# A decoder layer on one core: the order of work in 39 expert tiles, weights split one unit ahead, gate and up signalled apart

## What is computed

```
x = layernorm(x + self_attention(x))                  # 16 heads
x = layernorm(x + cross_attention(ctx, x))
X = x + attention(rmsnorm(x))
h2 = rmsnorm(X)                                       # 4096 tokens x 256
topw, topi = top_k(softmax(h2 @ router_w), 2)         # 2 of 8 experts for each token
shared = swiglu(h2, sh_gate, sh_up, sh_down)
spec   = sum over e of combine[:, e] * swiglu(h2, e_gate[e], e_up[e], e_down[e])
out = layernorm(x + X + shared + spec)
# swiglu(x, g, u, d) = (silu(x @ g) * (x @ u)) @ d ; g, u: 256 x 512, d: 512 x 256
```

## Time and profile before

| | |
|---|---|
| runs | 1156.73 us median of 3 (1155.41 to 1157.38) |
| profiled execution | 1154.84 us, span 1153.0 us |
| TensorE busy | 1076.8 us, 93% of the span |
| VectorE, ScalarE, GpSimd busy | 805.8, 620.1, 551.0 us |
| units 0 to 12 | 617.8 to 742.3 us of the span |
| tiles (units 13 to 51) | 742.3 to 1100.4 us |
| after the tiles | 1100.4 to 1153.0 us |

### The profile page before, as it was taken

How to read it: one execution, slowest core, us unless ns; L and a number is a source line. 1 busy time by engine, 2 the same in 40 slices (tenths; PEclk the granted TensorE clock), 3 DMA queues, 4 the chain that set the end, 5 groups by cost and what they waited for, 6 DMA issues and landing times. The chain is left out here.

```text
span 1153.0 us, 32693 instructions
## 1 busy us (share of the span) xinstructions
PE 1076.8 (93%) x13012; PEld 1011.7 (88%) x13012; DVE 805.8 (70%) x1367; ACT 620.1 (54%) x1266; POOL 551.0 (48%) x542
## 2 busy tenths in 40 slices
PE   3789999999999999999966999999999999999992
PEld 2678889989898989898865999999999999999992
DVE  1668778777778777788645644577777777777746
ACT  1244555555555555566544333466666666666635
POOL 4243334344343344434201477346666666666754
PEclk8999999999999999999986999999999999999996
DMA  7585455454654444541215422368878887878548
GB/s 211 101 192 106 94 95 107 114 115 91 131 111 91 120 108 74 103 71 35 93 38 167 165 102 97 125 202 230 239 232 236 231 226 219 224 233 230 139 76 244
DMA packets 294679, 167.73 MB, mean 145 GB/s; under 512 B 220688, under 2 KB 266000, under 8 KB 293648
## 3 DMA queue, kind: packets, MB, share of 16 engines
q1 hardware_dynamic: 278064, 141.05, 45.5%
q0 software_dynamic: 14880, 22.09, 9.4%
q10 hardware_dynamic: 1584, 2.49, 0.6%
HBM read 121.74 MB, written 54.15 MB: 153 GB/s over the span
## 5 line engine op out<-in xcount | busy, mean ns | idle before, releaser
L1580 POOL DMA_INDIRECT total_scratch<-kept_late,slot_meta x78 | 135.4, 1736 | 110.6 <-DMA total_scratch<-kept_late,slot_meta 58.5
L1450 DVE TENSOR_TENSOR prod<-kept_weights,up 128x512 f32<-128x512 f32 x110 | 75.2, 683 | 144.2 <-ACT kept_weights L1290 144.2
L1569 POOL TENSOR_TENSOR act_lo<-prod,act_hi 128x512 fp32r<-128x512 f32 x78 | 120.3, 1686 | 36.5 <-ACT act_hi L1297 36.5
L1297 ACT ACTIVATE act_hi<-prod 128x512 fp32r<-128x512 f32 x110 | 69.5, 632 | 111.1 <-DVE prod L1450 109.7
L1290 ACT ACTIVATE kept_weights<-gate 128x512 f32<-128x512 f32 x110 | 64.8, 589 | 110.6 <-PE up L1221 110.6
L678 ACT ACTIVATE p3t<-psum 128x512 f32<-128x512 f32 x128 | 68.8, 596 | 89.2 <-PE psum L527 89.2
L929 POOL TENSOR_TENSOR ctx_lo<-ctx_t,ctx_hi 128x512 fp32r<-128x512 f32 x16 | 20.6, 1288 | 139.8 <-ACT ctx_hi L588 139.8
L849 DVE TENSOR_REDUCE max<-psum 128x16 f32<-128x2048 f32 x32 | 73.3, 2292 | 18.2 <-PE psum L513 18.2
L368 PE MATMUL psum<-kept_room,x_hi 128*128 128x512 f32 (+1 forms) x256 | 62.4, 367 | 18.3 <-POOL x_lo L925 18.3
L1274 ACT ACTIVATE we_hi<-w_raw 128x1024 fp32r<-128x1024 f32 x78 | 77.7, 1044 | 0.0
L1221 PE MATMUL gate<-tok_hi,we_hi 128*128 128x256 f32 x312 | 67.7, 298 | 1.2 <-DVE we_lo L1434 0.7
(11 more groups left out here) (277 smaller groups left out, 3404.7 us busy)
## 6 DMA issues: line engine op xcount, KB each, us to landing
w_raw<-in_w_gate SPq DMA_DIRECT2D x26, 512.0 KB, 3.6
w_raw<-in_w_up SPq DMA_DIRECT2D x26, 512.0 KB, 4.5
w_raw<-in_w_down SPq DMA_DIRECT2D x26, 512.0 KB, 6.2
slots_scratch<-in_empty SPq DMA_DIRECT2D x39, 258.0 KB, 3.8
kept_weights<-slots_scratch SPq DMA_DIRECT2D x39, 258.0 KB, 6.0
raw_gate<-in_w_gate SPq DMA_DIRECT2D x13, 512.0 KB, 3.6
h_rows<-in_w_up SPq DMA_DIRECT2D x13, 512.0 KB, 4.5
h_rows<-in_w_down SPq DMA_DIRECT2D x13, 512.0 KB, 6.2
```

Of the source, the lines that this page charges most:

```text
L1297: act.activation(act_hi[:, n % 2, h * FH:(h + 1) * FH, :], prod[:, h, :].rearrange("p (f n) -> p f n", f=FH), ACT.Copy).then_inc(act_hi_do ...
L1450: dve.tensor_tensor(prod[:, h, :], silu[:, h, :], up[h][:, :], ALU.mult).then_inc(prod_done, 1)
L1569: pool.tensor_tensor(act_lo[:, n % 2, h * FH:(h + 1) * FH, :], prod[:, h, :].rearrange("p (f n) -> p f n", f=FH), act_hi[:, n % 2, h * FH: ...
L1580: pool.indirect_dma_start(out=scratch["total"], out_offset=bass.IndirectOffsetOnAxis(ap=slot_meta[:, i % METAS, j, 0:1].bitcast(I32), axis=0),
```

## The change

Four things change in `phase_b`, all in the order of the work or in what is signalled; no instruction that computes is added or removed.

1. `gate_up` now counts once after `gate` and once after `up` of each half. `silu_half` waits for the gate alone; `product` on DVE now waits for `up` itself, beside silu. All other users wait for the same event as before, by `up_at`.
2. All three weights of tile n + 1 are split during unit n. Before, kinds 0 and 1 were, and kind 2 in the tile's own unit.
3. Each engine's order in a tile unit is another: PE turns the next tokens after both halves, just before `down_unit(n - 1)`; ACT and DVE put a weight split between the other steps; DVE's `read_down` is that of unit n - 1 rather than n - 2, at the end of the unit; POOL adds tile i - 1 after both `routed_lo` of tile i, where it added tile i - 2 between them.
4. Unit 12, the last before the tiles, and unit 52, the first after them, have orders of their own: in unit 12 the turn of tile 0 moves behind `down_unit(11)`, and `down_unit(12)` is done right after it; in unit 52 the turn of unit 53 moves behind `down_unit(51)`.

```diff
@@ -1107,6 +1108,13 @@
             i = tile_of(n)
             return kind + 1 if i is None else 3 + 3 * i + kind + 1
 
+        def gate_at(k):
+
+            return 2 * k + 1
+
+        def up_at(k):
+            return 2 * k + 2
+
         totals = scratch["total"][0:P * B, :].rearrange("(p b) d -> p b d", p=P)
 
         def added_upto(i):
@@ -1221,7 +1229,7 @@
                                     mm = pe.matmul(bank[:, fi * UT:(fi + 1) * UT],
                                                    wp[:, kind, dk * DFF + f * P:dk * DFF + (f + 1) * P],
                                                    hp[:, n % 2, dk, :], start=(m == 1), stop=(m == 3 * DK))
-                    mm.then_inc(gate_up_ready, 1)
+                        mm.then_inc(gate_up_ready, 1)
 
                 def down_unit(n):
                     w_hi, w_lo = weights_of(n)
@@ -1241,15 +1249,30 @@
                 turn(0)
                 for n in range(UNITS):
                     gate_up(n, 0)
-                    if n + 1 < UNITS:
+                    if n < FIRST_TILE - 1:
                         turn(n + 1)
-                    if n == AFTER_TILES:
+                        gate_up(n, 1)
+                        if n == 2:
+                            pe.wait_ge(rank_read, 1)
+                        if n >= 1:
+                            down_unit(n - 1)
+                    elif n == FIRST_TILE - 1:
+
+                        gate_up(n, 1)
                         down_unit(n - 1)
-                    gate_up(n, 1)
-                    if n == 2:
-                        pe.wait_ge(rank_read, 1)
-                    if n >= 1 and n != AFTER_TILES:
+                        turn(n + 1)
+                        down_unit(n)
+                    elif n == AFTER_TILES:
                         down_unit(n - 1)
+                        if n + 1 < UNITS:
+                            turn(n + 1)
+                        gate_up(n, 1)
+                    else:
+                        gate_up(n, 1)
+                        if n + 1 < UNITS:
+                            turn(n + 1)
+                        if n > FIRST_TILE:
+                            down_unit(n - 1)
                     if n == 0:
                         pe.wait_ge(loaded, 16 * 3)
                         pe.wait_ge(ones_b_set, 1)
@@ -1268,7 +1291,7 @@
                     act.wait_ge(*((kept["loaded"], KEPT) if use == 0 else (raw_loaded[(use - 1) % 3], 48 * ((use - 1) // 3 + 1))))
                     if i is not None and i >= 2:
                         if kind < 2:
-                            act.wait_ge(gate_up_ready, 2 * (n - 2) + 2)
+                            act.wait_ge(gate_up_ready, up_at(2 * n - 3))
                         else:
                             act.wait_ge(down_ready, n - 1)
                     act.activation(w_hi[:, kind, :], raw_of(use)[kind], ACT.Copy).then_inc(w_hi_done, 1)
...
@@ -1284,7 +1307,7 @@
 
                 def silu_half(n, h):
                     k = 2 * n + h
-                    act.wait_ge(gate_up_ready, k + 1)
+                    act.wait_ge(gate_up_ready, gate_at(k))
                     if k >= 2:
                         act.wait_ge(prod_done, k - 1)
                     act.activation(silu[:, h, :], gate[h][:, :], ACT.Silu).then_inc(silu_done, 1)
@@ -1318,21 +1341,43 @@
                 route(None)
                 for kind in range(3):
                     split(0, kind)
-                for n in range(UNITS):
-                    i = tile_of(n)
-                    tile_next = n + 1 < UNITS and tile_of(n + 1) is not None
-                    silu_half(n, 0)
+                def split_next(n, kind):
+                    if n + 1 < UNITS and tile_of(n + 1) is not None:
+                        split(n + 1, kind)
+
+                def tokens_next(n):
                     if n + 1 < UNITS:
                         token_hi(n + 1)
-                    product_hi(n, 0)
-                    if i is not None:
-                        split(n, 2)
-                    if tile_next:
-                        split(n + 1, 0)
-                        split(n + 1, 1)
-                    silu_half(n, 1)
-                    route(n)
-                    product_hi(n, 1)
+
+                for n in range(UNITS):
+                    silu_half(n, 0)
+                    split_next(n, 0)
+                    if n < FIRST_TILE - 1:
+                        tokens_next(n)
+                        product_hi(n, 0)
+                        silu_half(n, 1)
+                        route(n)
+                        product_hi(n, 1)
+                    elif n == FIRST_TILE - 1:
+                        product_hi(n, 0)
+                        silu_half(n, 1)
+                        split_next(n, 1)
+                        product_hi(n, 1)
+                        tokens_next(n)
+                    elif n == AFTER_TILES:
+                        tokens_next(n)
+                        split_next(n, 1)
+                        product_hi(n, 0)
+                        silu_half(n, 1)
+                    else:
+                        product_hi(n, 0)
+                        silu_half(n, 1)
+                        tokens_next(n)
+                        split_next(n, 1)
+                        product_hi(n, 1)
+                    split_next(n, 2)
+                    if n == AFTER_TILES:
+                        product_hi(n, 1)
                     late = n - AFTER_TILES
                     if late >= 1:
                         normalize(range(NORMALIZED[late - 1], NORMALIZED[late]))
@@ -1445,6 +1490,7 @@
                 def product(n, h):
                     k = 2 * n + h
                     dve.wait_ge(silu_done, k + 1)
+                    dve.wait_ge(gate_up_ready, up_at(k))
                     if k >= 2:
                         dve.wait_ge(*low_products(k - 2))
                     dve.tensor_tensor(prod[:, h, :], silu[:, h, :], up[h][:, :], ALU.mult).then_inc(prod_done, 1)
@@ -1495,32 +1541,51 @@
                 for kind in range(3):
                     split_lo(0, kind)
                 choose_first()
-                for n in range(UNITS):
-                    i = tile_of(n)
-                    if n == AFTER_TILES:
-                        read_down(n - 2)
-                    product(n, 0)
-                    if 2 <= n < AFTER_TILES:
-                        read_down(n - 2)
+                def split_next(n, kind):
+                    if n + 1 < UNITS and tile_of(n + 1) is not None:
+                        split_lo(n + 1, kind)
+
+                def tokens_next(n):
                     if n + 1 < UNITS:
                         token_lo(n + 1)
-                    tile_next = n + 1 < UNITS and tile_of(n + 1) is not None
-                    if i is None:
+
+                for n in range(UNITS):
+                    product(n, 0)
+                    if n < FIRST_TILE - 1:
+                        if n >= 2:
+                            read_down(n - 2)
+                        tokens_next(n)
                         product_lo(n, 0)
+                        for part in ROUTING.get((n, 0), ()):
+                            part()
+                        product(n, 1)
+                        product_lo(n, 1)
+                        for part in ROUTING.get((n, 1), ()):
+                            part()
+                    elif n == FIRST_TILE - 1:
+                        split_next(n, 0)
+                        product_lo(n, 0)
+                        read_down(n - 2)
+                        product(n, 1)
+                        product_lo(n, 1)
+                        split_next(n, 1)
+                        read_down(n - 1)
+                        tokens_next(n)
+                        split_next(n, 2)
+                    elif n >= AFTER_TILES:
+                        tokens_next(n)
+                        product_lo(n, 0)
+                        if n == AFTER_TILES:
+                            read_down(n - 1)
+                        product(n, 1)
+                        product_lo(n, 1)
                     else:
-                        split_lo(n, 2)
-                    for part in ROUTING.get((n, 0), ()):
-                        part()
-                    if tile_next:
-                        split_lo(n + 1, 0)
-                        split_lo(n + 1, 1)
-                    if n == AFTER_TILES:
+                        split_next(n, 0)
+                        product(n, 1)
+                        tokens_next(n)
+                        split_next(n, 1)
                         read_down(n - 1)
-                    product(n, 1)
-                    if i is None:
-                        product_lo(n, 1)
-                    for part in ROUTING.get((n, 1), ()):
-                        part()
+                        split_next(n, 2)
 
                     late = n - AFTER_TILES
                     if late >= 2:
@@ -1558,7 +1623,7 @@
 
```

(13 more changed lines are left out.)

## The result

The changed kernel took 1177.2 us, the median of 4 runs (1173.8 to 1180.8), against 1156.8 (1155.4 to 1157.4, 4 runs) before: ratio 1.018, interval 1.016 to 1.020. Slower, where I had forecast 1152.9 and at most 1160.0. The profiled execution took 1175.1 us, span 1173.3, which is 20.3 more than before. The starts of the units say where. Up to unit 12 it is 2.0 us shorter, which I don't count as the change's: a second execution of the changed kernel (experiment 3) reached unit 12 at 733.4 us, the first at 730.0, the kernel before at 732.0. Entering the tiles (unit 12 to 14) takes 20.14 against 19.37, **+0.8**; the 38 units from 14 to 52 take 371.79 against 349.03, **+22.8**; what lies behind takes 51.4 against 52.6, **-1.2**.

What follows compares the result with a forecast made beforehand. TensorE was taken to bound the tile stretch, with 5.9 us to gain. Entering +1.0, tile stretch -3.5 and behind the tiles -1.3 sum to -3.8 us: forecast 1152.9 us, range 1149.5 to 1160.0.

Steps and rivals of the forecast that it cites:

- Entering the tiles: Units 12 to 14: 1.02 us wait at tile 0's turn goes, new 2.08 us before unit 14's gate; +1.0 us.
- The bound: Units 14 to 52: TensorE carries the stretch; 349.03 us against 343.1 without waits, so 5.9 us to gain.
- The count after gate: Additional counts in each unit's gate and up matmuls, priced at 0; by the skill's figure 2.9 us worse.
- The wait behind the pair: Tile units: VectorE's up split waits out GpSimd's two `act_lo`, then needs 1.1 us; 1.35 us late where both hold it.
- a residual of 2.4 us over the 38 units: Tile stretch: 0.4 us lost in every sixth unit to the up split's wait, leaving -3.5 us.
- Rival C: Tile units: both `act_lo` delay the up split in one unit of four, 9 or 10; +6.6 us, 1163.3 us; chance 0.17.
- rival A: Tile units: adds get ahead of the weight loads, all 5.9 us come; -6.2 us, 1150.5 us; chance 0.2.
- with 0 to 5 us of the stretch given back: The likeliest case's own range for the whole kernel, 1151.0 to 1154.3 us.
- Behind the tiles: From unit 52: last add at 9.75 us, not 11.11; waits of 0.61 and 0.66 us clear; -1.3 us.

Runs made afterwards that it cites:

- experiment 3: Changed kernel with silu waiting for both gate and up again: 1179.2 us, ratio 1.0212 to before; the unaltered changed kernel run beside it: 1176.8 us, 1.0187.
- experiment 8: Changed kernel with GpSimd's add between the two `act_lo` and, in unit 13, tile 1's turn between the halves: 1147.15 us, ratio 0.9929; again 1146.8, 0.9923.
- experiment 1: Changed kernel with the next up weight's split moved ahead of product 1 on VectorE and ScalarE: 1182.4 us on a slower chip, ratio 1.0019 to before.
- experiment 2: Changed kernel with GpSimd's add of tile i - 2 between the two `act_lo`, as before: 1175.7 us on a slower chip, ratio 0.9958 to before.
- experiment 5: Changed kernel without the adds of the tiles' rows and the waits for them: 1174.2 us on a slower chip, ratio 0.9956 to before.
- experiment 7: Kernel before with only GpSimd's order changed, both `act_lo` and then the add: 1219.2 us, ratio 1.0541 to before.

## Why the prediction was wrong

**The bound** was read rightly: TensorE, units of 9.0 without waits, about 6 us to gain. The 342.4 us without adds and 342.6 with experiment 8's order are my 343.1.

**The count after gate** at 0: right (0.9999 alone). The 2.9 us, an estimate from the figure of the Trainium skill ("TensorE: Matmul & The Clock Gate", The cost: per-tile semaphore tail), were not seen.

**The wait behind the pair** was priced rightly in kind: I had the phase (adds at t = 4.3, pair from 7.5, split asked at 8.4, ending at 11.8) and the trace has 4.3, 7.7, 8.2 and 11.9. Such a unit costs 1.6 to 2.0 us, where I had 1.35.

**The step that failed** is the one behind it: "But a wait moves the phase, the loads come later, and the next split goes in ahead. I take a residual of 2.4 us over the 38 units (0.4 us in every sixth)". The mechanism is right; what I mis-sized is how often it comes back. The wait does let the next split in between the two `act_lo`. But mostly it takes the phase only one unit away: the split that goes in on time gives the delay back, and the next unit, or the one behind it, has the bad phase again. So it came back in 15 of 38 units, for 14 of them 23.4 us together (1.67 each over a unit of 9.02) and 4.3 in the one of 13.31. Of these 4.3 the wait itself is only 2.5; behind it the granted clock was 0.50, 1.2 GHz, which I had not priced either. The row of TensorE, and the busy time of a stretch behind it:

```profile
1067.62 0.73 PE L1229 MATMUL up<-tok_hi,we_hi 128*128 128x256 f32 x2 [2.52 <-DVE we_lo_place L1479]
...
1069.10:1070.60 1.50, 1.50 (x9) 1.50 (x9) 0.40 (x2) 0.00 (x0) 1.50 (x1) 0.50 0.00 0
```

With unit 14's 1.6 (below) that is 29.3 us, where the stretch before had held 6.5 (349.0 - 342.5): +22.8. I had worked that phase out to 0.3 us, found it bad, and then priced it by the hope that it would not recur, without laying out the second unit and the third. Rival C was the case, with 15 units where I gave it 9 or 10, and a higher price of each; experiments 1, 2 and 5 show its cause three ways. Of rival A nothing came: adds mostly start at t = 3.6 to 5, nearly all of them 0.7 to 0.8 us behind the landing of the add before (the profile puts most of these waits down to `slot_meta`, but their times follow that landing). One line of the prediction doesn't add up, though the forecast doesn't use it: with 0 to 5 us of the stretch given back its sum gives 1151.4 to 1156.4, not 1151.0 to 1154.3.

**Entering the tiles.** +0.8 against +1.0. The wait at the turn of tile 0 is gone and one of 1.84 us, for which I had 2.08, stands before unit 14's gate. I did not price the clock, for it had stayed at 1.00 with a small wait in each unit; but those waits were of about 0.2 us. Here it fell: from the start of unit 14 the windows of after show it at 0.53 and 0.50, 1.2 GHz, after TensorE had idled 1.84 us:

```profile
748.32:750.16 1.84, 0.00 (x1) 0.00 (x1) 1.22 (x3) 1.80 (x4) 0.00 (x0) 1.00 0.45 105
750.16:751.98 1.82, 1.82 (x9) 1.82 (x10) 1.80 (x3) 1.45 (x2) 1.24 (x1) 0.53 0.37 99
751.98:753.50 1.52, 1.52 (x9) 1.52 (x9) 1.52 (x2) 0.46 (x1) 0.57 (x1) 0.50 0.05 11
753.50:755.00 1.50, 1.50 (x14) 1.50 (x14) 0.25 (x2) 1.09 (x2) 0.00 (x0) 0.94 0.00 0
```

Unit 14 took 10.61 us instead of 9.0, so entering costs 2.4 in all. Experiment 8 gives both back (stretch 344.2 to 342.6, unit 12 to 14 20.14 to 18.13).

**Behind the tiles**, -1.2 against -1.3, by the two waits named: the last add starts 9.81 us into unit 52 (I had 9.75), and the row of ScalarE that ended before with a wait of 0.66 runs through. GpSimd and ScalarE after:

```profile
1131.76 1.55 POOL L1645 DMA_INDIRECT total_scratch<-kept_late,slot_meta  x1 [5.04 <-DVE kept_late L1519]
...
1156.63 13.92 ACT L1327 ACTIVATE acc<-acc,shift,rstd_b 128x256 f32<-128x256 f32 x28 [1.85 <-POOL shift L1672]
```

## What to carry to other kernels

When a layout on paper puts two engines on the same resource at the same time, lay out the unit after the delayed one and the one after that, until the phase repeats; the price is that of the cycle, not of one unit. Where a slow instruction of an engine can close up work behind it that would otherwise come spaced, put it between that work and not ahead of it: here one line of GpSimd's order decided between 0.996 and 1.018, and, in the kernel before, between 1.000 and 1.054. And a signal that comes earlier, or a wait that goes, is worth only what the order behind it can use.

## What the runs showed of the hardware

A split on VectorE (two inputs, 128x1024) takes 1.21 to 1.23 us alone. While GpSimd only issues adds it takes the same: of 234 such splits, in the traces of nine runs, 228 took at most 1.23 and six 1.25 to 1.28. Asked for while an `act_lo` runs, it ends 1.07 to 1.10 us after it, as if it had not begun. Two `act_lo` whose recorded spans touch count as one, while a gap of 0.33 us between them let it in.

Behind an add it is otherwise. Where the record of `act_lo` begins 1.0 us after that of the add ahead of it, splits asked for 0.35 to 0.71 us before the recorded start of `act_lo` were held too (3.44 to 4.88 us), and those asked for 0.74 or more before it ran in 1.22 to 1.29. The longest wait of all, in unit 46, is of this kind: asked for at 1062.68, 0.71 us before the first of two `act_lo` that touch (1063.39 to 1066.47), the split took 4.88.

Without an add ahead, a split asked for 0.56 us before `act_lo` ran in 1.22; so did three of experiment 3 asked for 0.57 before an `act_lo` that began 1.4 us after the add. The Trainium skill, "SBUF — State Buffer", 🔬 SBUF: two separate sides, says that VectorE (with two inputs in SBUF) and GpSimd share a pair of ports under an exclusive lock, which whichever starts first keeps for its whole instruction. The ends behind a single `act_lo` agree with that. That a waiting split isn't let in between two that touch goes beyond it, and the starts behind an add don't agree: there the split was first by the record and yet held. What holds it no run here shows.

TensorE's granted clock: 35 idle times of 1.6 to 1.7 us in experiment 7, one a unit, left it at 1.00. Behind the wait ahead of unit 14 (1.84 to 2.27 us) it was 0.50 in all six profiled runs that had it. Of the eight waits of 2.2 to 2.4 us in experiment 3 four were followed by 0.50 and four were not. What decides it is not shown.

In after, the add at 851.56 was issued 1.2 us ahead of the next weight loads (852.72), the one at 842.48 right behind its tile's; they landed 6.4 and 6.9 us after their issue. Being in front of the loads brought an add little.

On one of the chips the kernels reached unit 12 at 756.1 to 760.8 us of the span, where on the others it was 730.0 to 733.4; the kernel before took 1180.2 us there and 1155.6 and 1155.8 on two others, so the change is no cause of it. The same window of experiment 2 there, and of after elsewhere:

```profile
670.00:680.00 10.00, 5.75 (x20) 4.52 (x21) 3.21 (x6) 1.95 (x4) 6.01 (x9) 0.57 0.22 79
```

```profile
670.00:680.00 10.00, 10.00 (x86) 10.00 (x86) 5.05 (x10) 4.09 (x9) 7.61 (x10) 1.00 0.30 104
```

TensorE ran 20 matmuls where 86 ran otherwise, with idle time that no engine or transfer released. What holds it up stays open.
